# A two-block transformer tower: expert weights split once in the first stage, expert loops written out, attention contexts turned by VectorE and a transfer

## The chip, the cores and the metric

One core of a Trainium2 chip runs the whole program. The metric is the device time of one execution in microseconds (us). Engines: PE is TensorE (matmuls; PEld its weight loads), DVE is VectorE, ACT ScalarE, POOL GpSimd, SP SyncE, which only issues transfers. Each engine runs its own instructions in order and waits at semaphores for others.

## The reference

Eight sequences of 1024 tokens (B = 8, S = 1024), width D = 128. In float32:

```python
emb = x @ W + pe                                      # tokens, 29 features each
# block 0: attention, 8 "heads" taken by reshape(B*8, S, 16), residual, layer norm
attn = softmax(q @ k.T * scale); ctx = attn @ v
n0 = layernorm(emb); x = emb + layernorm(ctx @ Wo.T + bo + n0) * gamma + beta
# block 0: per-sequence mixture of experts (8 experts, top 2), hidden 512
h  = gelu(x_norm @ w1[e] + b1[e]); eo = gelu(h @ w2[e] + b2[e]); x += g[b, e] * eo
# block 1: attention over blocks of 32 tokens (the same row of each block), projection
# block 1: per-token mixture of experts (8 experts, top 2), hidden 512
h  = gelu(x_norm @ W1[e] + b1[e]); y = h @ W2[e] + b2[e]; x += g[token, e] * y
```

## The kernel before, in words

The program is a chain of stages with a barrier between them: `embed_and_attend` (embedding and the first attention), `sequence_gates`, `sequence_experts`, `block_attention`, `plan_tiles` (sorting tokens into expert tiles), `token_experts`, `add_results`. The residual stream H stays in SBUF.

**First stage.** The batches (sequences) follow each other, and each is written out as 32 *bursts*; burst m handles two *units*. A unit is 1024 columns of exponentials: PE writes the scores of a unit to one of three PSUM pairs psS (two matmuls, L426), ACT takes the exponential (L343, 128 x 1024), and PE multiplies it by the values (four matmuls of 32 rows, L438) into the bank psO. Eight bursts make a *quarter*: one pair of heads is then complete in psO, DVE copies it out (`out_of_psum`, L643), and PE can use psO again. In the quarter after that, the pair is finished in three steps through the one other free bank, psA: PE transposes the copy (`turn`, L446), DVE divides by the sums (`divide`, L648, L650), PE transposes back (`turn_back`, L452), DVE copies (`evacuate`, L657), PE projects (`project`, L458), DVE adds the input (`add_input`, L664). At the same time the next batch is prepared by the twelve steps of the table STEPS, one after the bursts named there: E (embedding), T (transpose), q, k (products in three parts of split float32), N (norms that decide if a maximum is needed), v. They too go through psA, so that each use of psA waits until DVE has read the one before (`psA_free`). SP stores the split q and k to DRAM (`qparts`, `kparts`, L209) and loads them as the stacked operands qs and ks (six transfers for each, L215); a semaphore counts the whole batch. `guard` writes two more rows of qs (gparts, L238), sent by SP. `finish` (layer norm, residual, second norm) follows a half batch on DVE and POOL, by the tables UPPER and LOWER.

**Expert stages.** Both use `expert_items`. An *item* is 512 rows through one expert: PE transposes the rows (psX, L845), multiplies by w1 into four banks psH and by w2 into psY; each product is three matmuls (L69 to L71), because both operands are split in a high and a low part. ACT takes gelu twice (L807, L809), DVE subtracts to get the low part (L922), ACT writes y (L823), PE transposes it (L874) and DVE weighs it (L1154 or L1766). The expert's weights come raw in four transfers and DVE splits them: two casts (L62) and two subtractions (L64) for each expert load, in the midst of its other work. The first expert stage has 32 items (8 rounds of 4, two expert loads a round), the second 40 items with one expert load each; its rows come from the sorted queue (L1712) and its results leave by four indirect transfers of POOL an item (L1744). All rounds but the first and last run in a hardware loop on every engine.

Of the kernel before, what the change touches and what calls it, by code (L numbers as in the profile page):

```python
# [16 lines left out]
P = 128  # L17
# [90 lines left out]
def embed_and_attend(nc, H, ident, half, mean1, rstd1, score1, ins, B, S, D, NH):  # L108
# [12 lines left out]
    PIECES = ((0, 0, 0), (0, 1, 16), (1, 0, 32))  # L121
# [7 lines left out]
    def score_buffer(u):  # L129
# [7 lines left out]
    TURN, BACK, PROJECT = 1, 2, 3  # L137
# [5 lines left out]
    PSA_PAIR, PSA_EMBED = 3, len(STEPS)  # L143
    PSA_BATCH = PSA_PAIR * HP + PSA_EMBED

    with ExitStack() as ctx:
# [15 lines left out]
        qf = [[c.sb(f"{n}f{ch}", [D, CH]) for ch in range(CPB)] for n in "qk"]  # L162
# [12 lines left out]
        o_sb = c.sb("o_sb", [P, CH])  # L175
        stage = c.sb("stage", [P, HP * P], F32R)
        rden = c.sb("rden", [P, 4, 4])
        ctx_tm, ctxT = c.sb("ctx_tm", [P, 2, KT, DH]), c.sb("ctxT", [D, 2, P])
        res = [c.sb(f"res{p}", [P, TPC, D]) for p in range(2)]
        dq = [nc.dram_tensor(f"qparts{p}", [D, 2, 2, HALF], F32).ap() for p in range(2)]  # L180
        dk = [nc.dram_tensor(f"kparts{p}", [D, 2, 2, HALF], F32).ap() for p in range(2)]

# [4 lines left out]
         psA_free, cleared, normal_done, stream_done, qparts_done, kparts_done, qparts_out, kparts_out, stack_in, pre_qk, pre_max, gt_ps,  # L187
         gparts_done, guard_in, qk_done, exp_done, pv_done, o_evac, ht_ps, ctx_done, ct_ps, ctxT_done, staged,
         op_done, sq_done, n_ps, waited, qf_done, kf_done, unsafe_done) = (c.sem(n) for n in (
            "tok_in pe_in w_in wsplit x_in0 x_in1 emb_ps var_e root_e var_f root_f n0_done nt_ps nt_done q_ps k_ps v_ps "  # L190
            "psA_free cleared normal_done stream_done qparts_done kparts_done qparts_out kparts_out stack_in pre_qk pre_max gt_ps "
            "gparts_done guard_in qk_done exp_done pv_done o_evac ht_ps ctx_done ct_ps ctxT_done staged "
            "op_done sq_done n_ps waited qf_done kf_done unsafe_done").split())

        x_in = (x_in0, x_in1)
        N_W = 12
        STACK = 16 * 2 * 2 * len(PIECES) * CPB
# [7 lines left out]
        def redistribute(eng, b, par, kind, ch):  # L205
# [12 lines left out]
        def psA_uses(b, prior):  # L218

            return Tally(b * PSA_BATCH - PSA_PAIR) if prior else Tally(0)  # L220

# [6 lines left out]
        def _(sp):  # L228
# [36 lines left out]
            for ch in range(CPB):  # L265
                redistribute(sp, 0, 0, 0, ch)
# [1651 lines left out]
```

## Time and profile before

| what | us |
|---|---|
| median of 3 runs (lowest to highest) | 1564.57 (1563.72 to 1567.42) |
| the profiled execution: its own time | 1566.77 |
| its span in the trace | 1564.5 |
| first stage, to the last instruction of its work | 0 to 689 |
| first exponential / last copy out of psO | 61.7 / 669.5 |
| gates | 689 to 726 |
| sequence experts | 726 to 945 |
| block attention and tile plan | 945 to 1216 |
| token experts | 1216 to 1510 |
| adding the results | 1510 to 1564.5 |

Busy over the span: PE 1250.5 us (80%), DVE 989.6 (63%), ACT 1012.1 (65%), POOL 520.9 (33%). Times of rows below are microseconds from the span's start; the idle time in brackets stands ahead of an instruction, with what ended it.

### The profile page before, as it was taken

The numbers are of one execution on the slowest core, as the hardware profiler recorded it, in microseconds if no ns is written. First come the engines' busy times: TensorE is split into PE (matmuls) and PEld (weight loads), VectorE is DVE, ScalarE is ACT, GpSimd is POOL, SyncE is SP. The second block draws the span as 40 slices with busy tenths as digits, with TensorE's granted clock in tenths as the row PEclk, the third lists the DMA queues.
The fourth block names the chain that finished last, engine by engine and source line by source line (L and its number), as shares of the span: only waits on it lengthen the run. The fifth ranks groups of instructions, "written<-read, shape, count | busy, mean of one in ns | idle before, by whom it ended". The sixth has DMA issues, their size and how long they took to land. (4 is left out here: it accounts for less than half of the span.)

```text
span 1564.5 us, 30966 instructions
## 1 busy us (share of the span) xinstructions
PE 1250.5 (80%) x9689; PEld 826.3 (53%) x9689; DVE 989.6 (63%) x2772; ACT 1012.1 (65%) x1358; POOL 520.9 (33%) x456
## 2 busy tenths in 40 slices
PE   3599999999999999926999994888870699999930
PEld 2244444444444444414777773777760577777720
DVE  5256666666666664333777876788641589999932
ACT  0387778777778888902888883444410688888820
POOL 3212222222222221210000001278775066666654
PEclk9599999999999999967999996888855799999975
DMA  3542424242425252001111100011112455555519
GB/s 89 88 97 46 93 49 97 45 93 49 95 47 97 42 102 36 2 9 48 34 48 34 47 7 12 4 40 46 46 47 101 113 146 147 151 149 151 151 44 299
DMA packets 134465, 118.97 MB, mean 76 GB/s; under 512 B 30459, under 2 KB 112310, under 8 KB 134350
## 3 DMA queue, kind: packets, MB, share of 16 engines
q1 hardware_dynamic: 114798, 93.72, 26.5%
q0 software_dynamic: 9216, 16.94, 3.2%
q10 hardware_dynamic: 10336, 6.82, 2.2%
q8 instruction: 67, 1.10, 0.3%
q14 instruction: 48, 0.39, 0.1%
HBM read 76.61 MB, written 42.37 MB: 76 GB/s over the span
## 5 line engine op out<-in xcount | busy, mean ns | idle before, releaser
L343 ACT ACTIVATE a_probs<-a_psS 128x1024 f32<-128x1024 f32 x512 | 491.2, 1031 | 125.5 <-PE a_psS L426 98.4
L438 PE MATMUL a_psO<-a_probs,a_v 128*32 128x256 f32 x4096 | 282.5, 395 | 24.7 <-DVE a_o_sb L643 23.9
L807 ACT ACTIVATE f_g_hi<-f_psH,f_b_hid 128x512 fp32r<-128x512 f32 x288 | 200.6, 696 | 56.4 <-PE f_psH L71 49.6
L922 DVE TENSOR_TENSOR f_g_lo<-f_g,f_g_hi 128x512 fp32r<-128x512 f32 x288 | 197.7, 688 | 54.6 <-ACT f_g L809 52.5
L1744 POOL DMA_INDIRECT result<-f_out,f_idx x160 | 184.2, 1151 | 118.4 <-DVEq L1768 62.8
L426 PE MATMUL a_psS<-a_qs,a_ks 50*128 50x512 f32 x1024 | 193.8, 457 | 26.6 <-issue 12.4
L809 ACT ACTIVATE f_g<-f_psH,f_b_hid 128x512 f32<-128x512 f32 x288 | 199.8, 694 | 0.0
L438 PEld LDWEIGHTS a_psO<-a_probs,a_v 128*32 128x32 f32 x4096 | 108.7, 111 | 170.1 <-issue 89.2
L426 PEld LDWEIGHTS a_psS<-a_qs,a_ks 50*128 50x128 f32 x1024 | 79.2, 191 | 99.6 <-ACT a_probs L343 46.4
L69 PE MATMUL f_psH<-f_x_hi,f_w_lo 128*128 128x512 f32 x288 | 125.3, 435 | 2.9 <-DVE f_w_lo L64 2.6
L69 PE MATMUL f_psY<-f_g_hi,f_w_lo 128*128 128x512 f32 x288 | 117.1, 407 | 8.5 <-DVE f_w_lo L64 6.2
L1245 POOL DMA_INDIRECT queue<-all_row,all_idx x112 | 109.6, 978 | 32.9 <-issue 32.6
L71 PE MATMUL f_psH<-f_x_hi,f_w_hi 128*128 128x512 f32 x288 | 115.6, 401 | 0.0
L70 PE MATMUL f_psH<-f_x_lo,f_w_hi 128*128 128x512 f32 x288 | 115.3, 400 | 0.0
L71 PE MATMUL f_psY<-f_g_hi,f_w_hi 128*128 128x512 f32 x288 | 113.6, 394 | 0.0
L70 PE MATMUL f_psY<-f_g_lo,f_w_hi 128*128 128x512 f32 x288 | 113.4, 394 | 0.0
L279 POOL TENSOR_TENSOR a_rs_f<-a_veps_f,all_half 128x4 f32<-128x4 f32 x32 | 32.4, 1012 | 168.8 <-DVE a_veps_f L98 168.8
L1248 POOL MEMSET a_diag<- 128x1024 f32 x1 | 1.0, 951 | 248.3 <-POOLq L1099 248.3
L64 DVE TENSOR_TENSOR f_w_lo<-f_raw,f_w_hi 128x512 fp32r<-128x512 f32 x112 | 77.6, 693 | 8.4
L817 ACT ACTIVATE f_x_hi<-f_psX 128x512 fp32r<-128x512 f32 x56 | 33.6, 601 | 66.0 <-PE f_psX L845 66.0
L69 PEld LDWEIGHTS f_psY<-f_g_hi,f_w_lo 128*128 128x128 f32 x288 | 54.2, 188 | 34.8 <-issue 18.1
L71 PEld LDWEIGHTS f_psH<-f_x_hi,f_w_hi 128*128 128x128 f32 x288 | 55.2, 192 | 12.6
(296 smaller groups left out, 2152.7 us busy)
## 6 DMA issues: line engine op xcount, KB each, us to landing
f_raw<-W SPq DMA_DIRECT2D x80, 256.0 KB
a_qs<-qparts SPq DMA_DIRECT2D x96, 128.0 KB, 4.7
a_ks<-kparts SPq DMA_DIRECT2D x84, 128.0 KB, 4.7
f_rows<-queue SPq DMA_DIRECT2D x40, 260.0 KB, 2.7
qparts<-a_parts SPq DMA_DIRECT2D x16, 512.0 KB, 2.8
f_raw<-w SPq DMA_DIRECT2D x32, 256.0 KB, 2.6
kparts<-a_parts SPq DMA_DIRECT2D x14, 512.0 KB, 3.2
out_y<-result SPq DMA_DIRECT2D x8, 512.0 KB, 14.0
```

The costliest lines, as they stand in the source:

```text
L64: return nc.vector.tensor_tensor(lo, src, hi.bitcast(F32), ALU.subtract)
L69: nc.tensor.matmul(out, w_lo, x_hi, start=first, stop=False)
L70: nc.tensor.matmul(out, w_hi, x_lo, start=False, stop=False)
L71: return nc.tensor.matmul(out, w_hi, x_hi, start=False, stop=last)
L343: nc.scalar.activation(probs[u % NPR][:, :], psS[score_buffer(u)][:, :, :].rearrange("p a n -> p (a n)"), ACT.Exp).then_inc(exp_done, 1)
L426: last = nc.tensor.matmul(psS[score_buffer(u)][:, p, :], ks[par][64 * p:64 * p + KG, kt, hp * P:(hp + 1) * P], queries(par, hp, p, a), sta ...
L438: last = nc.tensor.matmul(psO[32 * g:32 * g + 32, a * HALF:(a + 1) * HALF], v[par][:, 2 * hp + p, kt, :], probs[u % NPR][:, cols:cols + HA ...
L807: nc.scalar.activation(g_hi[i][:, n, :], psH[n][:, :], ACT.Gelu, bias=b_hid[i][:, n:n + 1])
L809: nc.scalar.activation(g[:, n, :], psH[n][:, :], ACT.Gelu, bias=b_hid[i][:, n:n + 1]).then_inc(g_done, 1)
L922: nc.vector.tensor_tensor(g_lo[i][:, n, :], g[:, n, :], g_hi[i][:, n, :].bitcast(F32), ALU.subtract).then_inc(lo_done, 1)
L1245: pool.indirect_dma_start(queue, bass.IndirectOffsetOnAxis(ap=idx[n % NROW][:, k, t:t + 1], axis=0), row[n % NROW][:, k, t, :], None).then ...
L1744: pool.indirect_dma_start(result, bass.IndirectOffsetOnAxis(ap=idx[i][:, j:j + 1], axis=0), out[i][:, j, :], None, bounds_check=2 * B * S ...
```

## The change

1. **Contexts of the first stage.** `out_of_psum` is now a DVE transpose of 32 x 32 blocks out of psO. `divide` works on that and transposes back. The pair then goes through DRAM (four stores and a load on SP's queue, `spread`) to the layout that `project` wants. `turn`, `turn_back` and `evacuate` are gone from PE and DVE. `project` comes LATE = 2 quarters after its pair and stands ahead of the value matmuls of its burst.
2. **Steps.** STEPS has E, T, q, k at every second burst from 1 to 19; RESCUE goes from 26 to 22; the tables of `finish` and of the norm's application are new.
3. **Stack loads.** Four transfers in place of six for each of q and k, a semaphore for each half of a batch; POOL, not SP, sends the guard rows.
4. **Splitting.** In each batch, DVE splits four of the 32 weight matrices of both expert stages (after bursts 14, 20, 25, 30); POOL loads them and stores the parts to DRAM.
5. **Expert stages.** No splitting there. An expert's parts and biases (128 rows of 2053 floats) are one transfer into one of four buffers; all items are written out instead of looping.

```diff
-    STEPS = {0: ("E", 0), 4: ("E", 1), 6: ("T", 0), 8: ("q", 0), 12: ("k", 0), 14: ("T", 1), 16: ("q", 1), 20: ("k", 1),
-             22: ("N", 0), 24: ("N", 1), 28: ("v", 0), 30: ("v", 1)}
+    STEPS = {1: ("E", 0), 3: ("E", 1), 5: ("T", 0), 7: ("q", 0), 9: ("k", 0), 11: ("T", 1), 13: ("q", 1), 15: ("k", 1),
+             17: ("N", 0), 19: ("N", 1), 27: ("v", 0), 29: ("v", 1)}
-    RESCUE = 26
+    LATE = 2
+    SPLIT = {14: 0, 20: 1, 25: 2, 30: 3}
+    RESCUE = 22
-    UPPER = {3: "add_bias", 7: "normal", 10: "moments", 11: "second", 13: "score"}
-    LOWER = {21: "add_bias", 23: "normal", 26: "moments", 27: "second", 29: "score"}
-    APPLY = {1: 0, 5: 1}
+    UPPER = {2: ("moments", 0), 4: ("second", 0), 6: ("score", 0), 10: ("add_bias", 1), 12: ("normal", 1), 18: ("moments", 1), 23: ("second", 1),
+             25: ("score", 1)}
+    LOWER = {26: ("add_bias", 0), 28: ("normal", 0)}
+    APPLY = {2: 0, 8: 1}
...
+            def spread(pair):
+                sp.wait_ge(norm_done, pair + 1)
+                for p in range(2):
+                    for cc in range(2):
+                        row = 64 * p + 32 * cc
+                        sp.dma_start(dctx[pair % 2][64 * cc:64 * cc + 64, p, :].rearrange("(i d) t -> d i t", d=DH),
+                                     o_n[row:row + DH, :].rearrange("d (i t) -> d i t", t=P)).then_inc(ctx_out, 16)
+                sp.wait_ge(ctx_out, (pair + 1) * 4 * 16)
+                if pair:
+                    sp.wait_ge(op_done, pair)
+                sp.dma_start(ctxT[:, :, :], dctx[pair % 2]).then_inc(ctx_in, 16)
...
+                for q in range(CPB):
+                    if more:
+                        redistribute(sp, b + 1, 1 - par, 0, q)
+                        redistribute(sp, b + 1, 1 - par, 1, q)
+                    spread(b * HP + q)
+                spread(b * HP + 2)
...
             def project(pair):
-                pe.wait_ge(ctxT_done, pair + 1)
+                pe.wait_ge(ctx_in, (pair + 1) * 16)
...
-                nc.vector.tensor_copy(o_sb[:, :], psO[:, :]).then_inc(o_evac, 1)
+                nc.vector.transpose(o_t[:, :, :].rearrange("p k e -> p (k e)"), psO[:, :]).then_inc(o_evac, 1)
...
+            def split_weights(j):
+                dve.wait_ge(raw_in, (j + 1) * 16)
+                if j:
+                    dve.wait_ge(split_out, j * 16)
+                nc.vector.tensor_copy(split[:, 0, :], raw[:, :])
+                dve.drain()
+                nc.vector.tensor_tensor(split[:, 1, :], raw[:, :], split[:, 0, :].bitcast(F32), ALU.subtract).then_inc(split_done, 1)
...
+            def load_parts(m):
+                e = sp.value_load(tile_e[0:1, m:m + 1], min_val=0, max_val=E - 1)
+                if m >= NW:
+                    sp.wait_ge(y_done, m - NW + 1)
+                sp.dma_start(w[m % NW][:, :], parts[bass.ds(e, 1), :, :].rearrange("o p c -> p (o c)")).then_inc(w_in[m % NW], 16)
```

On PE, a pair's context between the bursts of the second quarter, before (a_psS are scores, a_psO the values' sums):

```order
L438 MATMUL a_psO<-a_probs,a_v 32x256 x8
L446 MATMUL a_psA<-all_ident,a_o_sb 128x128 x4
L426 MATMUL a_psS<-a_qs,a_ks 128x512 x4
L438 MATMUL a_psO<-a_probs,a_v 32x256 x8
L452 MATMUL a_psA<-all_ident,a_ctx_tm 128x128 x2
L426 MATMUL a_psS<-a_qs,a_ks 128x512 x4
L438 MATMUL a_psO<-a_probs,a_v 32x256 x8
L458 MATMUL a_psA<-a_w_raw,a_ctxT 128x128 x2
```

and at the border of the second and third quarter now, where all that PE does for a pair stands:

```order
L69 MATMUL a_psA<-a_nT_hi,a_wk_lo 128x512
L70 MATMUL a_psA<-a_nT_lo,a_wk_hi 128x512
L71 MATMUL a_psA<-a_nT_hi,a_wk_hi 128x512
L512 MATMUL a_psS<-a_qs,a_ks 128x512 x4
L531 MATMUL a_psA<-a_w_raw,a_ctxT 128x128 x2
L524 MATMUL a_psO<-a_probs,a_v 32x256 x8
```

Two of three uses of psA by a pair are gone, and the third has moved between scores and values, right behind the k product. On SP's queue of one batch before:

```order
L209 DMA qparts<-a_parts 128x1024
L215 DMA a_qs<-qparts 16x8x256 x6
L209 DMA kparts<-a_parts 128x1024
L215 DMA a_ks<-kparts 16x8x256 x6
L209 DMA qparts<-a_parts 128x1024
L215 DMA a_qs<-qparts 16x8x256 x6
L209 DMA kparts<-a_parts 128x1024
L215 DMA a_ks<-kparts 16x8x256 x6
L238 DMA a_qs<-a_gparts 1x32x128 x4
```

and the piece of it now that ends with the contexts of the first pair:

```order
L237 DMA kparts<-a_parts 128x1024
L248 DMA a_ks<-kparts 32x8x256
L248 DMA a_ks<-kparts 16x8x256
L248 DMA a_ks<-kparts 32x8x256
L248 DMA a_ks<-kparts 16x8x256
L288 DMA contexts<-a_o_n 16x4x128 x4
L293 DMA a_ctxT<-contexts 128x256
```

A pair's contexts are issued only after the k parts of the next batch have been stored, and are queued behind their loads. On DVE in the second expert stage, one item before (f_meta is the rows' index and gate, f_g_lo the low part of gelu):

```order
L1758 COPY f_meta<-f_rows 128x8
L922 TENSOR_TENSOR f_g_lo<-f_g,f_g_hi 128x512
L908 COPY f_b_hid<-f_rawb 128x4
L62 CAST f_w_hi<-f_raw 128x512
L64 TENSOR_TENSOR f_w_lo<-f_raw,f_w_hi 128x512
L922 TENSOR_TENSOR f_g_lo<-f_g,f_g_hi 128x512
L902 TENSOR_TENSOR f_x_lo<-f_psX,f_x_hi 128x512
L922 TENSOR_TENSOR f_g_lo<-f_g,f_g_hi 128x512
L915 COPY f_b_out<-f_rawb 128x1
L62 CAST f_w_hi<-f_raw 128x512
L64 TENSOR_TENSOR f_w_lo<-f_raw,f_w_hi 128x512
```

and the stage's first rows now:

```order
L1752 COPY f_meta<-f_rows 128x8
L941 TENSOR_TENSOR f_x_lo<-f_psX,f_x_hi 128x512
L1752 COPY f_meta<-f_rows 128x8
L941 TENSOR_TENSOR f_x_lo<-f_psX,f_x_hi 128x512
L1752 COPY f_meta<-f_rows 128x8
L946 TENSOR_TENSOR f_g_lo<-f_g,f_g_hi 128x512 x6
```

The six instructions of the splitting are gone, and the third item's f_meta now stands ahead of the first f_g_lo.

## Rows read from the trace of the kernel before

**Rows 1.** Stretch, us, busy PE, PEld, DVE, ACT, POOL, clock, DMA share, GB/s.

```profile
1216.00:1510.00 294.00, 271.80 (x1280) 211.26 (x1280) 248.01 (x560) 240.67 (x401) 180.31 (x156) 0.96 0.49 137
1522.00:1546.00 24.00, 0.00 (x0) 0.00 (x0) 6.13 (x5) 0.00 (x0) 11.98 (x6) 0.50 1.17 282
```

**Rows 2.** The same view: four quarters of batch 4, one of batch 7.

```profile
378.72:398.16 19.44, 18.33 (x194) 9.37 (x194) 12.34 (x47) 16.88 (x18) 3.02 (x3) 1.00 0.00 1
398.16:417.44 19.28, 17.39 (x180) 8.26 (x180) 15.52 (x36) 14.69 (x17) 7.37 (x6) 1.00 0.43 97
417.44:435.42 17.98, 17.05 (x178) 7.94 (x178) 10.36 (x23) 15.19 (x17) 2.70 (x3) 1.00 0.79 147
435.42:456.42 21.00, 18.32 (x186) 9.21 (x188) 11.55 (x37) 14.75 (x16) 5.22 (x5) 0.92 0.33 49
608.11:623.53 15.42, 15.06 (x170) 6.73 (x170) 4.34 (x15) 14.79 (x17) 1.01 (x1) 1.00 0.01 1
```

**Rows 3.** Timeline of PE in that second quarter: start, duration, instruction, idle before.

```profile
398.89 1.07 PE L438 MATMUL a_psO<-a_probs,a_v 128*32 128x256 f32 x16 [1.69 <-DVE a_o_sb L643]
...
407.69 0.71 PE L458 MATMUL a_psA<-a_w_raw,a_ctxT 128*128 128x128 f32 x4
408.33 0.73 PE L426 MATMUL a_psS<-a_qs,a_ks 50*128 50x512 f32 x4
...
409.99 0.50 PE L69 MATMUL a_psA<-a_nT_hi,a_wk_lo 128*128 128x512 f32 x1
...
410.89 0.73 PE L426 MATMUL a_psS<-a_qs,a_ks 50*128 50x512 f32 x4
...
412.56 0.73 PE L426 MATMUL a_psS<-a_qs,a_ks 50*128 50x512 f32 x4
...
414.22 0.66 PE L364 MATMUL a_psA<-all_ident,a_n 128*128 128x128 f32 x4
414.80 0.73 PE L426 MATMUL a_psS<-a_qs,a_ks 50*128 50x512 f32 x4
```

**Rows 4.** Timeline of DVE: the k step, and the instruction behind it.

```profile
411.00 0.75 DVE L521 TENSOR_SCALAR a_kf<-a_psA,a_bcol 128x512 f32<-128x512 f32 x1 [0.34 <-PE a_psA L71]
...
414.03 0.69 DVE L595 TENSOR_TENSOR a_res<-a_res,a_brow 128x512 f32<-128x512 f32 x1
```

**Rows 5.** Groups of DVE, 61.7 to 608.1: count, busy us, mean ns.

```profile
L560 DVE STREAM_TRANSPOSE a_worstT<-a_worst 32x64 f32<-32x64 f32 x7 | 1.6, 232 | 0.5
```

**Rows 6.** Timeline of SP's queue: a store of k and its loads.

```profile
197.93 0.34 SPq L209 DMA_DIRECT2D kparts<-a_parts  x1
201.54 2.67 SPq L215 DMA_DIRECT2D a_ks<-kparts  x6
```

**Rows 7.** Transfers by line: count, size of one, us from issue to landing.

```profile
a_qs<-a_gparts SPq DMA_DIRECT2D x32, 16.0 KB, 2.1
```

**Rows 8.** Timeline: the first scores, and the last pair's `add_input`.

```profile
60.91 0.79 PE L426 MATMUL a_psS<-a_qs,a_ks 50*128 50x512 f32 x2 [11.87 <-DMA a_qs<-a_gparts]
...
673.71 0.42 DVE L664 TENSOR_TENSOR a_res<-a_psA,a_n 128x256 f32<-128x256 f32 x1 [0.91 <-PE a_psA L458]
```

**Rows 9.** Timeline of ACT, sequence experts: one item's output, and four items later.

```profile
848.48 0.69 ACT L823 ACTIVATE f_y<-f_psY,f_b_out 128x512 f32<-128x512 f32 x1
...
874.54 0.69 ACT L823 ACTIVATE f_y<-f_psY,f_b_out 128x512 f32<-128x512 f32 x1
```

**Rows 10.** The same, token experts: the second item's output, and 36 items later.

```profile
1245.85 0.69 ACT L823 ACTIVATE f_y<-f_psY,f_b_out 128x512 f32<-128x512 f32 x1
...
1490.92 0.69 ACT L823 ACTIVATE f_y<-f_psY,f_b_out 128x512 f32<-128x512 f32 x1
```

**Rows 11.** Timeline of PE, token experts: 15 matmuls apart, then the transposes of y.

```profile
1341.89 0.39 PE L69 MATMUL f_psY<-f_g_hi,f_w_lo 128*128 128x512 f32 x1
...
1345.37 0.60 PE L874 MATMUL f_psT<-all_ident,f_y 128*128 128x128 f32 x4
1345.73 0.48 PE L69 MATMUL f_psH<-f_x_hi,f_w_lo 128*128 128x512 f32 x1
```

More of the change, by code:

```diff
@@ L477, in batch @@
                         embed_step(*STEPS[m], b + 1, 1 - par, psA[:, :])
-                    if r in (TURN, BACK, PROJECT) and (q or prior):
-                        pe.wait_ge(psA_free, uses.next())
-                        {TURN: turn, BACK: turn_back, PROJECT: project}[r](pair)
             pe.sem_inc(pv_done, NPR)
@@ L494, in _ @@
             rounds(batch)
-            uses = Tally((B - 1) * PSA_BATCH - PSA_PAIR + PSA_PAIR * HP)
-            for step in (turn, turn_back, project):
+            uses = Tally((B - 1) * PSA_BATCH - LATE + HP)
+            for pair in range(B * HP - LATE, B * HP):
                 pe.wait_ge(psA_free, uses.next())
-                step(B * HP - 1)
+                project(pair)
         @block.vector
@@ L837, in _, with turn_x @@
+        hidden(0)
+        for m in range(N):
+            if m + 1 < N:
+                hidden(m + 1, then=m + 2 if new_x(m + 2) else None)
+            output(m)
     @block.tensor
     def _(pe):
-        def turn_x(it, k):
-            rows_wait(pe, it, k)
-            j = items.x_of(it, k)
-            if not (isinstance(j, int) and j == 0):
+        def turn_x(m):
+            rows_wait(pe, m)
+            j = x_of(m)
+            if j:
                 pe.wait_ge(x_done, j)
             for i in range(TPC):
-                last = nc.tensor.transpose(psX[:, i * P:(i + 1) * P], rows(it, k)[:, i, 0:D], ident[:, :])
+                last = nc.tensor.transpose(psX[:, i * P:(i + 1) * P], rows(m)[:, i, 0:D], ident[:, :])
@@ L858, in second @@
[L858 to L865 removed]
+                w_wait(pe, m)
+                pe.wait_ge(x_done, j + 1)
@@ L892, in _ @@
-        for n in range(NB):
-            first(0, 0, n)
-        items.run(pe, body)
-        turn_y(items.rounds - 1, R - 1)
+        turn_x(0)
+        if new_x(1):
+            turn_x(1)
+        for n in range(NB):
+            first(0, n)
+        for m in range(N):
+            if new_x(m + 2):
+                turn_x(m + 2)
+            for n in range(NB):
+                if m + 1 < N:
+                    first(m + 1, n)
+                second(m, n)
+                if n == 2 and m:
+                    turn_y(m - 1)
@@ new lines, in _ @@
+        rows_next(dve, 0)
+        split_x(0)
+        rows_next(dve, 1)
+        if new_x(1):
+            split_x(1)
+        rows_next(dve, 2)
+        for n in range(NB):
+            low(0, n)
+        for m in range(N):
+            for n in range(NB):
+                if m + 1 < N:
+                    low(m + 1, n)
+                if n == 1 and new_x(m + 2):
+                    split_x(m + 2)
+                if n == 2 and m + 3 < N:
+                    rows_next(dve, m + 3)
+                if n == 3 and m:
+                    back(m - 1)
@@ L1096, in sequence_experts @@
     K = 2
+    PER = K * CPB
     assert NB == 4 and CPB == 2
```

609 lines of the change are left out of this document (273 added, 336 removed).

## The prediction
> **What bounds the kernel now.** I first split the span by stages (the table of times) and then asked, in the three stages that the change touches, which engine is never idle. The first stage takes 689 us, and the busy times by quarter show its pattern [rows 2]: PE is busy 17 to 18 us of a quarter, ACT 14.7 to 16.9. In a batch with no next batch to prepare, a quarter takes 15.4 us, and there ACT, busy 14.8, is the limit as much as PE, with 15.1 (the last window of [rows 2]). So the first stage is bound by PE as long as it prepares the next batch, and ACT's floor of about 15.4 a quarter lies not far below. Four quarters of batch 4 make 19.4 + 19.3 + 18.0 + 21.0 = 77.7 us, the pace of the seven batches that prepare another. In the timeline of PE the reader is to see two things: what a piece of work costs from start to start, and the waits for DVE [rows 3]. In the last quarter the granted clock is 0.92 on average, so part of it ran at 1.2 and not 2.4 GHz, after PE had waited for the decision on the maximum; the same work at full clock takes about 1.4 us less.
>
> Token experts take 294 us; PE is busy 272 of them, DVE 248, ACT 241 [rows 1]. An item takes (1490.92 - 1245.85)/36 = 6.81 us [rows 10]. In the sequence experts four items take 26.1 us [rows 9]. There too PE is the limit, and what is above its own work is waiting and loop borders.
>
> **The first stage, batch by batch.** PE's costs from start to start [rows 3]: a burst 414.22 - 412.56 = 1.66, so eight make 13.3; project 0.64; the q or k product 0.90; T 0.58. E, N and v I take at the q product's 0.9 (an estimate; they are four matmuls or fewer). What is left of the 15.4 us quarter, 15.4 - 13.3 - 0.6 = 1.5, is turn, turn_back and the wait for the copy [rows 2]; the change takes all three off PE, up to 6 us a batch.
>
> Need of PE by quarter after the change: first (E, E, T, q) 13.3 + 2.7 + 0.6 + 0.6 = 17.2; second (k, T, q, k) 17.2; third (N, N) 15.7; fourth (v, v) 15.7. ACT's floor is 15.4. Then DVE. In the second quarter it was busy 15.5 of 19.3 us [rows 2]. From it go the copy of the context, the moments, the second norm and the score, some 4.6 us; to it come the transpose back, the application of the norm, a bias group, a second q step and a splitting. An operation on 128 x 512 takes 0.7 and the three of a k step 3.0 from start to start [rows 4], which makes 0.7 + 1.1 + 2.1 + 3.2 + 1.1 = 8.2 (estimates by these rows). So DVE comes to 19.1 busy, and with some 1.2 of gaps to 20.3 us: **in the second quarter DVE becomes the bound**. In the other quarters it stays below 16.
>
> The DVE transpose of 128 x 512 has no row. Its nearest is the one of 32 x 64, 232 ns [rows 5]. If all of it grows with the columns, it is 1.9 us; if it grows like the other operations, it is 0.7, as the copy. A gain is excluded, since no other operation of that size is under 0.4. I take 0.7: other operations on 64 columns take about as long as this one, and they reach 0.7 at 512. At 1.9 each pair costs DVE 2.4 more, which is on the path in the second quarter alone: 7 x 2.4 = 17 us. The Trainium skill (Vector Engine (DVE) Microarchitecture Reference, section 3.8) says the transposer is pipelined to sustain one element per cycle and lane; by that the sum stays at 0.7 each.
>
> Then **the contexts' way through DRAM**. A small transfer lands 2.1 us after its issue [rows 7]; two in a row and five issues (about 0.45 each) are 6.5 us, against a distance of a quarter. But SP's queue stands in order, and the first pair's contexts come behind the k parts: from the start of the second quarter DVE needs 0.7 + 3.2 (q) + 2.0 (divide) + 1.1 + 3.0 (k) = 10.0, the k store to its loads takes 3.6 [rows 6], four loads 1.8, then 6.5: 21.9, and more if the contexts wait behind the loads' data. The project stands at 20.3 + 0.7 = 21.0, and it cannot start before DVE has read the k product anyway, at about 22.5. I put 1.5 us for that read and as much again for the late context: the third quarter becomes 15.4 + 3.1 = 18.5. The other three pairs have 4 to 9 us to spare. The first quarter 17.2, the fourth 16.0 (the burst before the copy has ACT's pace): 17.2 + 20.3 + 18.5 + 16.0 = 72.0; with 1.0 for half-clock stretches, which waits like these bring now as before, 73.0. Against 77.7: 4.7 less, times 7 = **-33**. The last batch has no preparation and is at ACT's floor: -1.
>
> **The splitting in it** is 4 x 1.2 us of DVE a batch, one in the second quarter (counted), three where DVE has room. Its transfers (256 KB in, 512 KB out, four times in 73 us) are hidden behind the stage; POOL, busy under 7.4 us a quarter [rows 2], issues them. If POOL got late with them, the roots of the norms would come late, and DVE waits for these.
>
> **Start and end of the stage.** The first scores waited 11.87 us for the guard rows, which SP issued behind all stack loads [rows 8]. Now POOL sends them and scores need half of the stacks: I expect them 7 us earlier. POOL then clears buffers and issues the biases' small transfers while the first batch waits for its roots; I count 3 us for that: -4 (between -9 and +2). At the end, the last `add_input` at 673.7, 4.2 after the copy [rows 8], now waits for transposes, divide and the DRAM way, 2.5 + 6.5 and a project: 10 us after it. **+6.** The stage: -33 - 1 - 4 + 6 = **-32**.
>
> **Sequence experts.** Fifteen matmuls take 3.48 us, 0.232 each; 24 make 5.57; four transposes 0.36 [rows 11]. An item is 5.57 + 0.36 + 0.1 of restart, four with two row transposes 24.9, against 26.1 [rows 9]: the loop border and the waits for split weights are the difference. 1.2 x 8 = 9.6 less; the first item starts about 1.5 later, since it waits for one of 1 MB instead of 256 KB. **-8.** This costs nothing else, as ACT needs 9 x 0.58 = 5.2 an item.
>
> **Token experts.** The same way, 5.57 + 0.36 + 0.40 + 0.12 = 6.45 for 6.81: 38 x 0.36 = -13.7. ACT, ten operations of 0.58 to 0.6, is close behind. The transfers of an item grow from 1.0 MB to 1.6 MB, 243 GB/s at 6.45 us; before the share was 0.49 at 137 GB/s, and the final load, with long rows, moves 282 GB/s [rows 1]. It fits, with little to spare. The start is worse: the third item's rows are issued behind four loads of 1.05 MB, and DVE stands at their copy ahead of the first low part. At 282 GB/s three loads and the rows are 12 us, so that the first item's output comes some 7 us later; the second item waited before for other things, and I take +4.6. **-9.** The Trainium skill (DMA: Bandwidth & Descriptors, Queues, rings and completion order) has an engine consume descriptors in ring order; by this rule the rows can't overtake and the +4.6 stays, without it the stage would come to -14.
>
> **Sum**: 1566.8 (the profiled execution's time) - 32 - 8 - 9 = **1518 us**. The profiled execution is 2.2 above the median of the runs, so the sum may be as much too high.
>
> **Rivals.**
> *DVE holds the whole batch back.* Beside the second quarter, DVE's lateness reaches psA steps and copies elsewhere (the 1.69 us wait in [rows 3] is such a one), and the batch stays at 76 to 77: 1518 + 3.5 x 7 = 1543. For it speaks that DVE's work is denser than PE's need, against it that three quarters have room.
> *Nothing stalls.* Contexts come in time and POOL's parts are cheap: batches of 69 to 70, at the sum of PE's needs: 1518 - 3.5 x 7 = 1494.
> *Expert stages don't gain.* What ends PE's waits there is ACT, and an item stays at 6.8 and 26.1 for four: 1518 + 17 + 4.6 = 1540. Against it: the longest waits end with split weights and with rows.
> *Slower: the contexts' way.* If stores and loads of the contexts wait behind the stacks' and the splits' data, every project stands, and PE and ACT with it. The gain of 49 us is used up when the way takes 7 us more than counted in each of the seven batches, 29 in place of 22 from the start of the second quarter; at 10 more the time is 1518 + 70 = 1588. For it: one queue in order, four stores and a load a pair. Against it: DMA is busy 43% in that quarter [rows 2].
>
> **How the numbers follow.** The forecast has a chance of 0.58 (own range 1500 to 1536), the DVE rival 0.15, nothing stalls 0.12, experts without gain 0.09, slower 0.06. The transposer's upper bound (+17) and the start's (+6) lie within 1543. 1485 to 1555 leaves out the slower rival and the far ends. A measurement of this kernel can tell about 0.3%, 5 us, from no change. Faster by more than that: all but the slower rival and a tail of the others, 0.92; within 0.02; slower 0.06.
>
> **What would show it.** Quarters of 17, 20, 18.5 and 16 between the transposes out of psO, with DVE busy over 19 in the second; an idle PE of about 3 us before the first pair's project; the transpose at 0.7; first exponential near 55 to 58; items 6.45 apart in the last stage with the first output later after its rows than before. I would be wrong if the third quarter held a long wait for the contexts, or if DVE's load showed in all four.

## The result, and the profile after

The changed kernel is **slower**: 1604.5 us (1598.0 to 1613.1, 4 runs) against 1566.0 for the kernel before on the same chip, a ratio of 1.0242 (95% interval 1.0218 to 1.0267). The forecast was 1518. The profiled execution took 1605.77 us, with a span of 1603.8, 39.3 more than the span before.

| part of the span | before, us | after, us | difference | predicted |
|---|---|---|---|---|
| first stage, to its last `add_input` | 673.7 | 719.2 | +45.5 | -32 |
| to the first output of the sequence experts | 743.5 | 791.2 | +2.2 more | +1.5 |
| its 31 further outputs | 198.3 | 200.8 | +2.5 | -9.6 |
| to the first output of the token experts | 295.2 | 300.2 | +5.0 | +4.6 |
| its 39 further outputs | 264.1 | 248.2 | -15.9 | -13.7 |

The sum is +39.3. The token experts did what was forecast, and 77 of the 88 us between forecast and measurement lie in the first stage. Its quarters, as in [rows 2] (stretch, its length, busy PE, PEld, DVE, ACT and POOL, clock, DMA share, GB/s; from transpose to transpose out of psO):

```profile
413.00:435.30 22.30, 19.02 (x181) 8.72 (x177) 19.85 (x38) 16.33 (x17) 8.65 (x7) 0.92 0.55 126
435.30:454.10 18.80, 15.43 (x164) 6.61 (x164) 10.44 (x30) 13.37 (x15) 6.63 (x10) 0.91 0.85 201
454.10:478.40 24.30, 18.51 (x180) 9.08 (x180) 13.07 (x32) 15.19 (x17) 6.24 (x6) 0.86 0.28 81
478.40:497.50 19.10, 18.07 (x191) 9.38 (x191) 13.64 (x49) 15.96 (x17) 4.23 (x5) 1.00 0.21 63
664.60:679.60 15.00, 14.43 (x164) 6.25 (x164) 7.69 (x21) 14.71 (x17) 6.40 (x6) 1.00 0.16 51
```

The second, third, fourth and first quarter stand here in this order: 22.3, 18.8, 24.3 and 19.1, where the prediction has 20.3, 18.5, 16.0 and 17.2. Only the third came as forecast. Where the last batch prepares nothing, a quarter takes 15.0 for the 15.4 of before. Over the batches that prepare another, the medians are 22.5, 19.1, 24.7 and 18.8, so this batch is a usual one. What PE's projection waited for, over the stage (one line's own view):

```profile
L531 PE MATMUL a_psA<-a_w_raw,a_ctxT x128: 274/377/582, 102.6 to 718.7; 128*128 128x128 f32 x128
its engine sat idle before it (us, times) until:
  DMA a_ctxT<-contexts: 69.5, 14
  issue: 59.1, 20
  DVE a_kf L596: 20.2, 5
  DVE a_qf L596: 19.3, 12
  DVE a_res L734: 16.7, 2
```

14 of the waits, two in each of seven batches, end with the load of a context: this is the mechanism of the slower rival. PE's and SP's timelines show one batch (start, duration, instruction; "xN" is N instructions from this start on, in brackets the idle time before):

```profile
437.45 0.68 PE L531 MATMUL a_psA<-a_w_raw,a_ctxT 128*128 128x128 f32 x4 [3.67 <-DMA a_ctxT<-contexts]
...
454.10 0.73 PE L512 MATMUL a_psS<-a_qs,a_ks 50*128 50x512 f32 x4
460.56 1.19 PE L531 MATMUL a_psA<-a_w_raw,a_ctxT 128*128 128x128 f32 x4 [5.73 <-DMA a_ctxT<-contexts]
461.69 1.94 PE L524 MATMUL a_psO<-a_probs,a_v 128*32 128x256 f32 x16
```

```profile
423.33 0.34 SPq L237 DMA_DIRECT2D kparts<-a_parts  x1
427.54 1.76 SPq L248 DMA_DIRECT2D a_ks<-kparts  x4
429.35 3.34 SPq L288 DMA_DIRECT2D contexts<-a_o_n  x4
435.34 0.34 SPq L293 DMA_DIRECT2D a_ctxT<-contexts  x1
435.73 0.43 SPq L237 DMA_DIRECT2D qparts<-a_parts  x1
439.59 1.78 SPq L248 DMA_DIRECT2D a_qs<-qparts  x4
441.41 0.43 SPq L237 DMA_DIRECT2D kparts<-a_parts  x1
447.86 1.76 SPq L248 DMA_DIRECT2D a_ks<-kparts  x4
449.67 2.89 SPq L288 DMA_DIRECT2D contexts<-a_o_n  x4
458.51 0.34 SPq L293 DMA_DIRECT2D a_ctxT<-contexts  x1
```

The second pair's k parts were ready at 439.1 and its context at 441.1 (VectorE's L729). The k store was issued at 441.41, right behind four q loads, and its loads could go only 6.45 us later; [rows 6] had 3.6. SP stood at that point, so the context stores went out at 449.67, 8.6 us after their data were ready, and took until 458.51, with four k loads issued right ahead of them. The context was in SBUF 25.2 us after the quarter's start, and the quarter had lasted 18.8.

The cost goes on behind the wait: the projection takes 1.19 us instead of 0.68 and the values' products 1.94 instead of the 1.07 of [rows 3]. The granted clock of this quarter is 0.86 on average: after PE had stood idle for 5.73 us it was 0.50 from 460.5 to 463.6, the lower level (1.2 GHz), and 1.00 again from 466.0 on.

### The profile page after: what moved, and what is told of

Its sections match the earlier page's. It is cut to its first block and busy times, and to the rows that moved or that the text cites. A ratio compares the mean times of both kernels' runs of the same rounds, so it can differ in the third digit from the quotient of the medians.

```text
span 1603.8 us, 27058 instructions
## 1 busy us (share of the span) xinstructions
PE 1230.4 (77%) x9497; PEld 816.6 (51%) x9497; DVE 931.9 (58%) x2500; ACT 1001.4 (62%) x1358; POOL 582.2 (36%) x552
## 5 line engine op out<-in xcount | busy, mean ns | idle before, releaser
L946 DVE TENSOR_TENSOR f_g_lo<-f_g,f_g_hi 128x512 fp32r<-128x512 f32 x288 | 198.3, 690 | 170.4 <-ACT f_g L857 167.7
L524 PE MATMUL a_psO<-a_probs,a_v 128*32 128x256 f32 x4096 | 294.9, 409 | 0.3 <-ACT a_probs L427 0.3
L854 ACT ACTIVATE f_g_hi<-f_psH,f_w 128x512 fp32r<-128x512 f32 x288 | 201.6, 700 | 53.0 <-PE f_psH L71 39.1
L857 ACT ACTIVATE f_g<-f_psH,f_w 128x512 f32<-128x512 f32 x288 | 201.5, 700 | 0.0
L69 PE MATMUL f_psH<-f_x_hi,f_w 128*128 128x512 f32 x288 | 125.7, 436 | 5.2 <-DMA f_w<-experts 4.3
L71 PE MATMUL f_psH<-f_x_hi,f_w 128*128 128x512 f32 x288 | 115.3, 400 | 0.0
L70 PE MATMUL f_psH<-f_x_lo,f_w 128*128 128x512 f32 x288 | 115.2, 400 | 0.0
L70 PE MATMUL f_psY<-f_g_lo,f_w 128*128 128x512 f32 x288 | 113.9, 396 | 0.0
L69 PE MATMUL f_psY<-f_g_hi,f_w 128*128 128x512 f32 x288 | 113.9, 395 | 0.0
L71 PE MATMUL f_psY<-f_g_hi,f_w 128*128 128x512 f32 x288 | 113.6, 394 | 0.0
L531 PE MATMUL a_psA<-a_w_raw,a_ctxT 128*128 128x128 f32 x128 | 29.4, 366 | 86.1 <-DMA a_ctxT<-contexts 69.5
L395 POOL DMA_DIRECT2D experts<-a_split x32 | 19.4, 607 | 156.1 <-DVE a_split L743 156.0
L531 PEld LDWEIGHTS a_psA<-a_w_raw,a_ctxT 128*128 128x128 f32 x128 | 22.1, 245 | 98.7 <-issue 59.1
```

Of the source, the lines that this page charges most:

```text
L69: nc.tensor.matmul(out, w_lo, x_hi, start=first, stop=False)
L70: nc.tensor.matmul(out, w_hi, x_lo, start=False, stop=False)
L71: return nc.tensor.matmul(out, w_hi, x_hi, start=False, stop=last)
L524: last = nc.tensor.matmul(psO[32 * g:32 * g + 32, a * HALF:(a + 1) * HALF], v[par][:, 2 * hp + p, kt, :], probs[u % NPR][:, cols:cols + HA ...
L531: last = nc.tensor.matmul(psA[:, p * P:(p + 1) * P], ctxT[:, p, :], w_raw[:, 3, :], start=True, stop=True)
L854: nc.scalar.activation(g_hi[i][:, n, :], psH[n][:, :], ACT.Gelu, bias=bias(m, n))
```

## What the experiments were to decide

Theory A: the order of SP's queue makes the contexts late. B: the transfers of the splitting slow every other transfer. C: VectorE is too dense, and its lateness would take the place of the waits. The measure for the first stage is the start of its last transpose out of psO, 669.5 us before (there a copy) and 709.1 after.

The experiments ran on chips that the record numbers 1, 3 and 4; that of the first comparison has no number there and is called the first chip. On chips 1 and 3 the kernel before takes 1626 to 1629 us, on chip 4 1563.7. I had not expected that, and traced the kernel before on chip 3 too.

> The kernel before, traced on the chip of the experiments if it is met again (it needs 1626 to 1629 us there, 1566 on the first chip). The changed kernel took 47 us more there between the last output of the sequence experts and the first of the token experts, and 0.1 to 0.15 us more for a token item. If that is the chip and not the change, the kernel before shows 340 to 350 us there in place of 295, an unchanged first stage with its last copy at 669 to 670, and token items of 6.85 to 6.95 us.

Measured: the last copy at 671.0, so the first stage is the same. From the last output of the sequence experts to the first of the token experts it took 340.0 us (295.2 on the first chip), as expected, and a token item 7.23 (6.81), more than I expected. The changed kernel, on chip 1:

> The changed kernel itself, beside its variants on one chip, since the chip of the last runs needed 4% more for the kernel before, all of it behind the first stage. If that chip is met again: 1654 to 1660 us, 1.016 to 1.024 of the kernel before; the first stage's last transpose out of psO at 709 us, as in the first profile.

It took 1652.0 us, 1.0166 of before on that chip (1.0118 to 1.0215), with the last transpose at 702.2, 7 us earlier than expected, and a token item of 6.56. So on the slower chips the change gains more in the token experts (26.6 us over the 39 further outputs, from chip 3 to chip 1, for 15.9 on the first chip), and the ratio is smaller. Below, whole times are given as ratios to the kernel before on the same chip, and the first stage by its last transpose. A third trace of the changed first stage is in the run of the expert stages' order below, which leaves that stage as it is: 709.8 on chip 3. So the changed stage scatters by 7.6 us over three traces on three chips, and where a variant ran on chip 3 I compare it with the 709.8.

## SP's order, and what the splitting costs

`spread` is cut in two, `spread_out` (the four stores, L288) and `spread_in` (the load, L293):

```diff
                 for q in range(CPB):
+                    pair = b * HP + q
                     if more:
                         redistribute(sp, b + 1, 1 - par, 0, q)
-                        redistribute(sp, b + 1, 1 - par, 1, q)
-                    spread(b * HP + q)
+                        if q == 0:
+                            spread_out(pair)
+                        store_parts(sp, b + 1, 1, q)
+                        if q:
+                            spread_out(pair)
+                        spread_in(pair)
+                        load_parts(sp, b + 1, 1 - par, 1, q)
+                    else:
+                        spread(pair)
```

> SP's order alone is changed: in each half of the q and k work the stores of a context are issued before the k loads (for the first pair before the k store too) and its load before the k loads. Theory A, the queue's order: PE's waits for a context (3.7 and 5.7 us a batch in the changed kernel, 69.5 us over the stage) come from SP standing at the k store's landing. They fall below 1 us each, the half-clock stretches behind them go too, a batch takes 73 to 75 us in place of 84, and the time is 1525 to 1545 us. Theory B, contention: the transfers of the splitting make every transfer slow (a k store lands after 4.2 to 6.4 us, 3 before), so a context is late in any order; the waits stay over half, the time is above 1575. Theory C, VectorE: its queue is too dense, the contexts' waits only hide that; waits for DVE take their place and a batch stays at 80 or more, 1580 us or more.

Measured on chip 3: 1601.3 us, 0.9838 of the kernel before there (0.9792 to 0.9884), where the changed kernel has 1.0166 (on chip 1). The expectation was written for the first chip; 0.9838 of its 1566.0 would be 1541 us (an estimate from the ratio), in theory A's range. The last transpose came at 647.7, 62.1 us earlier than with the changed first stage on the same chip. The view of the projection's line (L544 here):

```profile
L544 PE MATMUL a_psA<-a_w_raw,a_ctxT x128: 275/275/583, 95.6 to 657.4; 128*128 128x128 f32 x128
its engine sat idle before it (us, times) until:
  DVE a_kf L609: 43.4, 14
  DVE a_qf L609: 19.3, 12
  DVE a_res L747: 16.7, 2
  issue: 8.6, 18
  DMA a_ctxT<-contexts: 2.0, 1
```

The waits for contexts fell to 2.0 us by an order of issue alone, from 58.1 on the same chip and 69.5 on the first. The projection's median fell from 377 to 275 ns, and the granted clock between first and last transpose rose from 0.92 to 0.97, so most stretches at the lower clock went too. Theory A holds for these 62.1 us. But 43.4 us of waits for VectorE's read of the k product took their place, and a batch takes 75.5 to 77.2, not the 73 to 75 that A had: theory C has a part in it. What VectorE does there (timeline of the changed kernel, with GpSimd's beside it):

```profile
430.75 1.77 DVE L629 TENSOR_TENSOR a_parts<-a_qf,a_parts 128x512 fp32r<-128x512 f32 x1
432.44 1.53 DVE L741 CAST a_split<-a_raw 128x512 fp32r<-128x512 f32 x1
434.04 1.37 DVE L743 TENSOR_TENSOR a_split<-a_raw,a_split 128x512 fp32r<-128x512 f32 x1
435.34 0.70 DVE L719 STREAM_TRANSPOSE a_o_t<-a_psO 128x512 f32<-128x512 f32 x1
436.20 0.75 DVE L596 TENSOR_SCALAR a_kf<-a_psA,a_bcol 128x512 f32<-128x512 f32 x1 [0.17 <-issue]
```

```profile
430.68 1.28 POOL L354 TENSOR_TENSOR a_res<-a_res,a_brow 128x512 f32<-128x512 f32 x1 [0.31 <-issue]
432.12 1.57 POOL L356 TENSOR_TENSOR all_H<-all_H,a_res 128x512 f32<-128x512 f32 x1
433.64 1.22 POOL L344 TENSOR_TENSOR a_qsq<-a_qf 128x512 bf16<-128x512 f32 x1
```

A splitting takes 2.9 us here and not 1.2. In the changed kernel's trace the copies and the subtractions with no elementwise work of GpSimd beside them, 16 of each, took 0.38 to 0.43 and 0.69 us; of the 16 with such work beside them, all but two took 0.68 to 1.53 and 1.37 to 1.64. The k product waited in psA meanwhile. The next two take the splitting out, in either order of SP.

> The splitting of the expert weights is taken out of the first stage (both VectorE's operations and GpSimd's transfers); behind the stage the raw weights are copied into both parts, so that the experts compute something else and the time from there on is not comparable. Only the first stage is read. Theory A: the contexts are late all the same, since SP's order is as it was; the quarters with a wait keep over 3 us of it, a batch takes 80 to 82 us. Theory B: a k store lands after 3 us again, the contexts' waits fall to 1 to 2 us, a batch takes 75 us. Theory C: with 4.8 to 7 us of VectorE's work gone, a batch falls by 5 or more, without a change of the contexts' way.

> Both: SP's new order and no splitting in the first stage (the experts compute something else, and only the first stage is read). Against the kernel with SP's new order alone it prices the splitting: theory A and the prediction say 1 to 2 us a batch, since only one of four splittings stands in the quarter where VectorE is the limit: 72 to 73 us a batch. If VectorE and GpSimd hold each other up at the memory port (a split's copy took 1.53 us next to GpSimd's operations, 0.43 alone), it is 3 us or more a batch.

Measured, both on chip 3: last transposes at 680.2 and 618.3. With SP's old order a batch takes 78 to 82 us and the waits for contexts are 44.8 us in 14, 3.2 on average: theory A had over 3 and 80 to 82, and theory C's fall of 5 us a batch came out as 4. Without splitting and with the contexts ahead a batch takes 71.6 to 72.0. The k store's way did not get shorter without the splitting's transfers (6.2 us to landing, median of six, against 5.5 in the changed kernel), which is against theory B as I had put it. What differs is what is issued right ahead: in the changed kernel the k loads go 3.8 to 4.7 us after the first half's k store and 5.9 to 8.5 after the second half's, which stands right behind four q loads.

On this one chip the two causes can be set side by side. Leaving the splitting out gains 29.6 us in SP's old order (709.8 to 680.2) and 29.4 with the contexts ahead (647.7 to 618.3). Two runs asked by what it costs 29 us with the contexts ahead.

```diff
-    SPLIT = {14: 0, 20: 1, 25: 2, 30: 3}
+    SPLIT = {18: 0, 22: 1, 26: 2, 30: 3}
```

> SP's new order (as in e1_contexts_ahead) and the four splittings of a batch at bursts 18, 22, 26 and 30 in place of 14, 20, 25 and 30, so that none lies in the quarter where VectorE is the limit. Theory D: the splitting costs 4 to 5 us a batch (28.8 and 29.3 us over the stage in the two comparisons) because VectorE is late there, 2.05 us a splitting in place of the 1.2 I counted; moved out, a batch takes 72 to 73.5 us (75.9 with the old places), and the kernel gains 15 to 25 us against e1_contexts_ahead. Theory F: it costs so much because its transfers slow the others; then the places don't matter, and a batch stays at 75 to 77.

> SP's new order, splittings at their old places, with VectorE's two operations each but without GpSimd's load and store; behind the stage the raw weights are copied into both parts, so the experts compute something else, and only the first stage is read. Theory D: a batch takes 75 to 77 us, as with the transfers, since VectorE has the same work. Theory F: it falls to 71.7, as without any splitting.

Measured, both on chip 1: with the splittings moved 1573.3 us, 0.9675 of before (0.9653 to 0.9697), the last transpose at 624.4; without their transfers but at the old places 643.3. The view by tile has them all in one line each (duration in ns, minimum, median and maximum, then the first and last start). These are the changed kernel on chip 1, its first stage on chip 3, contexts ahead on chip 3, contexts ahead with splittings moved on chip 1:

```profile
L719 DVE STREAM_TRANSPOSE a_o_t<-a_psO x32: 702/716/718, 76.3 to 702.2; 128x512 f32<-128x512 f32 x32
```

```profile
L719 DVE STREAM_TRANSPOSE a_o_t<-a_psO x32: 702/716/718, 77.0 to 709.8; 128x512 f32<-128x512 f32 x32
```

```profile
L732 DVE STREAM_TRANSPOSE a_o_t<-a_psO x32: 701/707/718, 76.7 to 647.7; 128x512 f32<-128x512 f32 x32
```

```profile
L732 DVE STREAM_TRANSPOSE a_o_t<-a_psO x32: 703/716/718, 76.3 to 624.4; 128x512 f32<-128x512 f32 x32
```

Theory D holds: with the contexts ahead it is VectorE's time in the one dense quarter that costs. Its work alone, without the transfers, keeps 25 of the 29 us (643.3 against 618.3), and 20 to 23 of them come back when it stands elsewhere (624.4 here and 627.2 in the version with all orders below, against 647.7; chips 1 and 3, which differ by an unknown amount in this stage). The wait for the k product fell from 43.4 us to 7.7.

Then the same places under SP's old order, to see whether the two causes add up:

> The changed kernel with its own order of SP, and the four splittings moved to bursts 18, 22, 26 and 30. It asks whether the two causes are independent: with the contexts ahead, moving the splittings gained 23 us of the first stage. If they add up, the last transpose out of psO comes 20 to 25 us earlier than the changed kernel's 702 to 709, at 680 to 687. If VectorE's lateness was hidden under the wait for the context, moving them gains less than 10, 695 or later.

Measured on chip 3: 700.2, against 709.8 on that chip and 702.2 on chip 1. **Moving does not add up**: it gains 2 to 10 us here, no more than the scatter of the changed stage, and 20 to 23 with the contexts ahead. The medians of the quarters show where the gain goes. The second quarter falls from 22.4 us to 19.5, as VectorE has less to do there, and the third rises from 19.4 to 23.8; the waits for contexts over the stage stay at 58 us. Leaving the splittings out, though, gained 29.6 in this order too. Two more runs took one half of them away each.

> The changed kernel, SP's order as it was, with VectorE's splittings but without GpSimd's loads and stores of them; behind the stage the raw weights are copied into both parts, so only the first stage is read (last transpose out of psO: 702 in the changed kernel, 680 without any splitting, 700 with the splittings only moved). Moving them did not help where the contexts are late, taking them away did. Theory G: while PE waits for the contexts, what counts of the splitting is how its transfers delay the chain of k parts and contexts; without the transfers the last transpose is at 680 to 686. Theory H: VectorE's own time decides here too, wherever it is put; then it stays at 696 to 703.

> The complement: the changed kernel with GpSimd's loads and stores at the old places, while VectorE only signals and splits nothing (zeros are stored as parts, and only the first stage is read). Theory G: the last transpose out of psO stays at 697 to 705. Theory H: 680 to 688. If both halves are needed, each of the two runs shows about half of the 22 us.

Measured on chip 4: 670.2 without the transfers, 708.8 with the transfers alone. Both lie outside their windows (680 to 686 and 697 to 705), but on theory G's side by far: with the transfers alone the stage is as long as the changed one. So where the contexts are late, the splitting costs through its transfers (768 KB each, four a batch), and VectorE's time is hidden under that wait. SP's timeline shows one thing that the transfers slow. Without them, the second pair's stores and load in the same order of SP (chip 4, no transfers):

```profile
430.01 1.84 SPq L288 DMA_DIRECT2D contexts<-a_o_n  x4
435.11 0.34 SPq L293 DMA_DIRECT2D a_ctxT<-contexts  x1
```

From the first of these stores to the load it is 5.10 us here and 8.84 in the batch shown above. The medians of this stretch over seven batches are 8.8, 7.7 and 7.8 in the three traces of the changed stage, 8.1 with the splittings moved and 8.0 with the transfers alone; without the transfers they are 5.8, and 6.3 with no splitting at all. So theory B was wrong for the k store in this order and right for the second pair's context stores. These 2 us a batch would make about half of the 29.6 us (an estimate, if all of them are on the path); where the rest arises was not followed up. The third quarter's DMA share of 0.85 above, with 201 GB/s, has this traffic in it (0.79 and 147 before, [rows 2]). All of it in one table, one trace for each number, its chip in brackets:

| last transpose out of psO, us | SP's old order | contexts ahead |
|---|---|---|
| splitting as changed | 709.1 (first), 702.2 (1), 709.8 (3) | 647.7 (3) |
| splittings moved | 700.2 (3) | 624.4 (1), 627.2 (1) |
| VectorE's part alone | 670.2 (4) | 643.3 (1) |
| transfers alone | 708.8 (4) | not run |
| no splitting | 680.2 (3) | 618.3 (3) |

One cell stays open: with VectorE's part alone and the old order the stage is 10 us shorter than with no splitting at all, on another chip. There the second pair's context is in SBUF 21.3 us after its transpose out of psO (median), and 25.3 with no splitting. VectorE's delay shifts the stores against each other; whether that is the cause wasn't tried. In the changed kernel's first trace a batch takes 79.8 in one place and 87.3 in another, so the pace is unsteady where contexts are late; with the contexts ahead it is 75.5 to 77.2.

## The expert stages

A pair of items in the sequence experts took 13.25 us (6.63 an item), and half of what the forecast had for four would be 12.45. PE waited for the pair's rows `f`, which VectorE writes behind the low part before (timeline of PE, then of VectorE):

```profile
889.25 0.39 PE L71 MATMUL f_psY<-f_g_hi,f_w 128*128 128x512 f32 x1
890.23 0.66 PE L889 MATMUL f_psX<-all_ident,f_f 128*128 128x128 f32 x4 [0.58 <-DVE f_f L1152]
890.64 0.48 PE L69 MATMUL f_psH<-f_x_hi,f_w 128*128 128x512 f32 x1
```

```profile
888.45 0.69 DVE L946 TENSOR_TENSOR f_g_lo<-f_g,f_g_hi 128x512 fp32r<-128x512 f32 x1 [0.61 <-ACT f_g L857]
889.06 1.11 DVE L1152 TENSOR_SCALAR f_f<-all_H,all_mean,all_rstd 128x128 f32<-128x128 f32 x4
```

From the last product of an item to the transpose is 0.98 us, where two products stand 0.23 apart: 0.75 lost, eight times in the 106 us that I looked at. The edit:

```diff
-                if n == 2 and m + 3 < N:
+                if n == (1 if per_x > 1 else 2) and m + 3 < N:
                     rows_next(dve, m + 3)
...
-            for m in range(1, NW):
-                load_parts(m)
-            for m in range(2, NW):
-                load_rows(m)
+            load_parts(1)
+            load_rows(2)
+            load_parts(2)
+            load_parts(3)
+            load_rows(3)
```

> The first stage is as in the changed kernel; two orders in the expert stages are changed. In the sequence experts VectorE prepares the next chunk's rows (f) one low part earlier, since PE waits 0.58 us for them in each pair of items, with 0.75 between its matmuls: if that is what keeps a pair at 13.25 us instead of the predicted 12.45, a pair takes 12.5 and the stage 10 to 12 us less; if the later low part then holds PE, a pair stays at 13.2. In the token experts the third item's rows are loaded behind two experts' parts and not four: the first output comes 3 to 5 us earlier, and the time falls by as much. Together 1588 to 1592 us; if neither decides, 1604.

`per_x > 1` is true in the sequence experts alone. Measured on chip 3: 1641.4 us, 1.0073 of before (1.0047 to 1.0099), where the changed kernel has 1.0166 (chip 1). ACT's outputs four items apart, and the two at the border of the stages:

```profile
866.67 0.69 ACT L870 ACTIVATE f_y<-f_psY,f_w 128x512 f32<-128x512 f32 x1
...
891.59 0.69 ACT L870 ACTIVATE f_y<-f_psY,f_w 128x512 f32<-128x512 f32 x1
...
981.39 0.69 ACT L870 ACTIVATE f_y<-f_psY,f_w 128x512 f32<-128x512 f32 x1 [2.32 <-PE f_psY L71]
...
1325.17 0.82 ACT L870 ACTIVATE f_y<-f_psY,f_w 128x512 f32<-128x512 f32 x1
```

Four items take 24.92, and the forecast had 24.9; the 31 further outputs take 189.6 us for 200.8. From the last sequence output to the first token output it is 343.8. That stretch also holds other stages and lies between 344.5 and 348.8 in four variants on the same chip that keep the old order of loads, so I read the gain nearer by: from the issue of the token experts' first rows to the first output it is 21.4 us, with the old order 25.5 to 27.4 in those four, 25.8 in the changed kernel on the first chip, and 21.0 in the kernel before. So the new order gives 4 to 6 us back, about what the start had lost.

All three orders in one kernel:

> The three new orders together: contexts ahead of the k loads, splittings moved, and the two orders in the expert stages (VectorE's rows one low part earlier in the sequence experts, where items went from 6.63 to 6.23 us; the third item's rows behind two experts' parts in the token experts). The effects add up, since the stages follow each other: 61 + 20 + 12.7 + 5, some 98 us less than the changed kernel, 0.955 to 0.965 of the kernel before on the same chip. If theory F holds, 0.970 to 0.975.

Measured on chip 1: **1561.1 us, 0.9602 of the kernel before** (0.9576 to 0.9628), and faster than the changed kernel on the same chip by 5.5% (91 us; I had expected 98). The last transpose stands at 627.2, where the forecast amounts to 669.5 - 33 - 1 - 4 = 631.5, and the outputs of four sequence items 24.91 apart (782.47 and 807.38). By this version the plan of the change is sound, and the places of transfers in SP's queue and of work in VectorE's took its gain away. On the first chip this version was not run.

## Why the prediction was wrong

- **The contexts' way: the step that failed.** The mechanism was named and put on the first pair alone, and there it came out: 24.4 us from the quarter's start to the projection for a forecast of 21.9 and more, a wait of 3.67 for 3.1. The sentence that failed is "The other three pairs have 4 to 9 us to spare". The second pair's context stands behind a second k chain, which I had not followed through the queue. I took 3.6 us from the k store to its loads out of [rows 6], where the last q load had been issued 3.4 us before it; right behind four q loads it was 6.45. And the context stores issued behind k loads were through 6.0 and 8.8 us after the first of them was issued (429.35 to 435.34, 449.67 to 458.51), where 3.0 suffice with nothing ahead (397.76 to 400.76). The fourth quarter took 24.3 for 16.0. Putting the contexts ahead gave 62.1 us back on one chip.
- **The chance of the slower rival**, 0.06, was too low. Its threshold was right in kind: it needed 7 us more than counted in a batch. I held a DMA share of 43% in that quarter [rows 2] against it. The share speaks of how full the transfer engines are, and what decided most was that SP stood in order at a semaphore (62.1 us); the splitting's transfers, which I had called hidden behind the stage, lengthened the same way.
- **The splitting: a term mis-sized.** Counted as 1.2 us a batch on the path, measured as 29 us over the stage, 4 a batch, in either order of SP. With the contexts ahead this is VectorE's time: the duration that I took was that of the operation without GpSimd beside it, 1.1 for the two, and in the dense quarter it was 2.9. With the contexts late it is the transfers.
- **VectorE as the bound of the second quarter** was right: 19.85 us busy for 19.1 forecast, 22.3 us long for 20.3. With the contexts ahead and the splitting elsewhere this quarter takes 19.0 to 19.6, in two batches of the version with all orders 20.9 and 21.8.
- **The transposer** was right: 0.70 to 0.72 us for 128 x 512, as the copy's 0.67 to 0.69. The Trainium skill (Vector Engine (DVE) Microarchitecture Reference, section 3.8) says that the transpose is pipelined to sustain one element per cycle and lane; the traces agree, at the duration of a copy.
- **PE's need** was 1.2 to 1.9 us too low in the first quarter: 18.4 to 19.1 in every variant, forecast 17.2. An E step is eight matmul records and takes 1.08 from start to start (482.39 to 483.47), not 0.9, and PE waits 1.0 for the low part of T. With nothing late a batch takes 71.7, and my sum for that was 72.0: here terms too low and too high cancel out.
- **Start and end of the stage**: the first exponential came 6.1 us earlier (55.6), forecast 4; the last `add_input` 10.1 us behind the last transpose (719.20 and 709.09), forecast 10.
- **Sequence experts**: forecast -9.6 for the items, measured +2.5. The sum of PE's own work was right, and the wait for `f` was not in it: in the kernel before, the waits of PE in a stretch of eight such pairs end with split weights (2.6 us in eight), none with `f`. With the rows earlier the forecast value came out.
- **Token experts**: an item 6.46 for 6.45 forecast, the start 5.0 later for 4.6. The +4.6 was a choice below the 7 us that the prediction worked out, so that this close is in part luck. The Trainium skill (DMA: Bandwidth & Descriptors, Queues, rings and completion order) says that descriptors are consumed in ring order, though a later one may finish its write before an earlier one. That loading the third item's rows behind two experts' parts in place of four gives 4 to 6 us back agrees with it.
- **Where the sum hit by luck**: the third quarter came as forecast, 18.8 for 18.5, though its wait of 3.67 for the context was one of two such waits a batch, of which the forecast had only this one.

## What to carry to other kernels

When a result is sent through DRAM by an engine that issues in order, write down the whole queue of one period with the wait of each entry, and follow every transfer through it, not the first alone: an entry behind a "stored, now load" wait is late by that round trip, whatever the transfer engines have free. Time such a round trip with what is issued just ahead of it. And price work that is moved onto a busy engine by the place where it lands: the same four splittings a batch cost 29 us with one of them in the dense quarter and 6 to 9 with all of them elsewhere. While another wait was longer, moving them gained little, and their cost, though of the same size, came by their transfers; so a cause must be tested again once a longer wait is gone. Compare such variants on one chip, or know how the unchanged stage scatters: against a trace of another chip the two gains of leaving the splitting out would read 22 and 29 us and not 29.6 and 29.4.

## What the hardware showed that I had not expected

- A copy of 128 x 512 on VectorE that takes 0.38 to 0.43 us takes up to 1.53, and a subtraction of 0.69 up to 1.64, in the presence of GpSimd's elementwise work on SBUF. That the two hold each other up is read from the overlap in the traces; GpSimd's work wasn't taken away to test it.
- Chips differ by 4% on the kernel before (1566 on the first and 1563.7 on chip 4, 1626 to 1629 on chips 1 and 3), with the same first stage to 1.5 us between the first chip and chip 3. The time lies between the expert stages (295.2 and 340.0) and, for the kernel before, in a token item (6.81 and 7.23). The changed kernel's item differs less, 6.46 and 6.56. Why was not looked into.
- A k store of 512 KB landed after 3.0 us in the kernel before and after 4.6 to 6.6 us in the changed kernel and its variants (medians of six or seven), where every second one stands right behind four loads on the same queue.
- Four stores of 32 KB and their landing took 3.0 us with nothing issued ahead, 6.0 and 8.8 right behind four loads of 128 and 256 KB.
